# The last sum of a graph and expert layer: terms read in rows, the base kept in SBUF, the last two experts added by TensorE

## The reference

```python
xn = _layernorm(x)                                     # x: 625 rows of 512
x = x + gnn(xn, edges, ...) + mix(xn, ...)             # 10625 edges; linear attention, 8 heads
h = _layernorm(x)
x = x + ffn(h, ...)
# ffn: 64 experts, the 6 best of each row, and 2 shared experts
shared = sum over 2 of silu(h @ sWg) * (h @ sWu) @ sWd
top_w, top_i = top_k(softmax(h @ Wr), 6); top_w /= sum(top_w)
gate[n, top_i[n]] = top_w[n]
routed = sum over e < 64 of (silu(h @ Wg[e]) * (h @ Wu[e]) @ Wd[e]) * gate[:, e:e+1]
return shared + routed + h
```

## Time and profile before

| | us |
|---|---|
| time, median of 3 runs | 1015.66 |
| lowest and highest of them | 1013.46, 1018.88 |
| time of the profiled execution | 1019.58 |
| its span | 1017.5 |
| TensorE busy | 895.9 (88% of the span) |
| VectorE busy | 548.1 (54%) |
| ScalarE busy | 256.0 (25%) |
| GpSimd busy | 268.2 (26%) |

### The profile page before, as it was taken

How to read it: one execution, slowest core, us unless ns; L and a number is a source line. 1 busy time by engine, 2 the same in 40 slices (tenths; PEclk the granted TensorE clock), 3 DMA queues, 4 the chain that set the end, 5 groups by cost and what they waited for, 6 DMA issues and landing times. The chain is left out here.

```text
span 1017.5 us, 20833 instructions
## 1 busy us (share of the span) xinstructions
PE 895.9 (88%) x7497; PEld 589.3 (58%) x7497; DVE 548.1 (54%) x1623; ACT 256.0 (25%) x573; POOL 268.2 (26%) x265
## 2 busy tenths in 40 slices
PE   1599998897878298999999999999999989999991
PEld 1355555564544196676556566766676765656660
DVE  7997987978798986323324333334233332333216
ACT  2111101121130132333322322333233322322331
POOL 4543321334300102222222222222222322222211
PEclk9699999999989789999999999999999999999996
DMA  8856454565428951889979999999988999999976
GB/s 276 287 207 207 158 186 171 207 207 208 166 63 279 373 206 57 319 303 367 405 290 334 359 383 413 390 387 361 405 307 332 353 400 398 365 374 366 402 289 262
DMA packets 76929, 300.68 MB, mean 296 GB/s; under 512 B 13730, under 2 KB 14119, under 8 KB 58548
## 3 DMA queue, kind: packets, MB, share of 16 engines
q1 hardware_dynamic: 57256, 254.21, 65.9%
q0 software_dynamic: 17280, 38.48, 10.5%
q10 hardware_dynamic: 2252, 6.06, 1.7%
HBM read 290.26 MB, written 26.62 MB: 311 GB/s over the span
## 5 line engine op out<-in xcount | busy, mean ns | idle before, releaser
L1202 DVE TENSOR_TENSOR arena<-arena 128x288 f32 (+1 forms) x640 | 236.3, 449 | 37.8 <-remote 24.5
L1826 PE MATMUL bank<-arena,low 128*64 128x256 f32 x2048 | 241.6, 383 | 2.0 <-issue 2.0
L1667 PE MATMUL bank<-arena,multi 128*64 128x256 f32 x1296 | 162.0, 400 | 44.0 <-DVE arena L1202 32.6
L1826 PEld LDWEIGHTS bank<-arena,low 128*64 128x64 f32 x2048 | 141.0, 137 | 75.6 <-issue 12.4
L1851 PE MATMUL bank<-arena,low 128*64 128x256 f32 x1392 | 161.6, 379 | 1.1 <-ACT low L980 1.1
L1667 PEld LDWEIGHTS bank<-arena,multi 128*64 128x64 f32 x1296 | 99.5, 144 | 102.2 <-issue 44.2
L743 POOL DMA_INDIRECT low<-xr_d,idx x64 | 90.2, 1409 | 238.7 <-DVE place L1433 177.6
L747 POOL DMA_INDIRECT y_d<-low,place x64 | 68.5, 1070 | 262.3 <-ACT low L987 181.8
L1851 PEld LDWEIGHTS bank<-arena,low 128*64 128x64 f32 x1392 | 101.3, 137 | 50.3 <-ACT low L980 1.3
L987 ACT ACTIVATE low<-bank,gcol 64x256 f32<-64x256 f32 x174 | 82.1, 472 | 105.0 <-PE bank L1851 103.9
L687 POOL DMA_INDIRECT arena<-xn_d,ssel x79 | 90.3, 1143 | 38.2 <-issue 21.8
(11 more groups left out here) (214 smaller groups left out, 710.9 us busy)
## 6 DMA issues: line engine op xcount, KB each, us to landing
arena<-in_L_ffn_Wg_dram SPq DMA_DIRECT2D x64, 1024.0 KB
arena<-in_L_ffn_Wu_dram SPq DMA_DIRECT2D x64, 1024.0 KB
arena<-in_L_ffn_Wd_dram SPq DMA_DIRECT2D x64, 1024.0 KB
arena<-in_edge_attr_dram SPq DMA_DIRECT2D x88, 256.0 KB
arena<-y_d SPq DMA_DIRECT2D x5, 1250.0 KB, 6.8
sums_d<-arena ACTq DMA_DIRECT2D x18, 256.0 KB, 3.2
arena<-sums_d SPq DMA_DIRECT2D x4, 896.0 KB
arena<-in_L_mix_W_qkv_dram SPq DMA_DIRECT2D x2, 1024.0 KB, 18.1
```

What stands on the lines that cost most here:

```text
L1202: return dve.tensor_tensor(prod[:, buf, 0:n, EXT * p:EXT * p + EXT], x1[b][:, 0:n, bass.ds(i1, EXT)], x2[b][:, 0:n, bass.ds(i2, EXT)], ALU ...
L1667: ins = pe.matmul(bank[2 * b + c // 2][64 * h:64 * h + 64, 256 * (c % 2):256 * (c % 2) + 256], pair[:, pairs, i, :], prod[:, buf, i, 256 * ...
L1826: ins = pe.matmul(out_bank[64 * h:64 * h + 64, w * HF:(w + 1) * HF], xgT[:, b, k, 64 * o:64 * o + 64], gu[:, slot, w, k, h * HF:(h + 1) * HF],
```

## The change

- The base is neither stored nor loaded: `base_d` is gone. The first add reads `x_sb` and term 0 and writes `total`. Terms, total and output are handled by rows: 125 partitions x 5 tiles x 512 floats, in pieces of 2,048 bytes, each transfer in two DMAs (112 and 13 partitions).
- The scatters stop after expert 61 (`KEPT` = 2). The rows of experts 62 and 63 stay in `yy`. As they would have gone to terms 4 and 5, which then have rows that nothing writes, these two terms are set to zero in DRAM by SP in windows 6 and 7 of the first part.
- For each of the two experts VectorE makes a table `marks` of 128 x 625 ones and zeros (row `p` has a one where `idx[p]` is the token). At the end TensorE multiplies each table's five parts by `yy`, adding both experts in five banks; VectorE adds the banks to `total` before the last term.
- Term 4 now needs no scatter after that of expert 61. Term 5 goes to the buffer of term 0 and so waits for the first add. Buffers move accordingly.
- ScalarE clears rows 64 to 127 of both `yy` buffers ahead of the loop.
- The branch for overflow batches, not taken here, is adapted.

```diff
+TILE = TT * D
+KEPT = 2
-    m["terms"] = [arena[:, a:a + FLAT] for a in (4 * GU, 4 * GU + FLAT, 0, GU, 2 * GU, 3 * GU)]
+    m["terms"] = [arena[0:TR, a:a + TILE].rearrange("p (t d) -> p t d", t=TT)
+                  for a in (4 * GU, 4 * GU + TILE, 0, TILE, 2 * TILE, 4 * GU)]
+    m["zeros"] = low[:, 7728:7978]
+    m["marks"] = xT[:, 0:KEPT * N].rearrange("p (j n) -> p j n", j=KEPT)
+        FINAL_BANK = (7, 0, 1, 3, 2)
+        ENDS = ((0, 2), (2, 4), (4, TT))
...
+            def blank_term(i):
+                flat = y_d[i * N:(i + 1) * N, :].rearrange("n d -> (n d)").rearrange("(p j c) -> p j c", p=128, c=250)
+                sp.dma_start(flat, zeros[:, None, :].to_broadcast([128, 10, 250])).then_inc(s_blank, 16)
...
+                if w in (6, 7):
+                    blank_term(w - 2)
...
             def load_term(i):
-                rows = flat(y_d[i * N:(i + 1) * N, :])
-                if i < TOPK - 1:
-                    sp.dma_start(terms[i], rows).then_inc(s_term[max(i - 1, 0)], 16)
-                else:
-                    for j, (a, b) in enumerate(((0, HALF), (HALF, FLAT))):
-                        sp.dma_start(terms[i][:, a:b], rows[:, a:b]).then_inc(s_term[i - 1 + j], 16)
+                rows = y_d[i * N:(i + 1) * N, :].rearrange("(t p) d -> p t d", t=TT)
+                for a, b in PARTS:
+                    sp.dma_start(terms[i][a:b], rows[a:b]).then_inc(s_term[i], 16)
...
-                if e == FIRST_DONE - 1:
-                    store_base()
-                if e == FIRST_DONE + 1:
-                    sp.wait_ge(s_based, 32)
-                    sp.dma_start(total, flat(base_d)).then_inc(s_basef, 16)
...
-            for i in range(2, TOPK):
+            for i in (2, 3):
                 scattered(FIRST_DONE + i)
                 load_term(i)
+            load_term(TOPK - 2)
+            sp.wait_ge(s_added, 1)
+            load_term(TOPK - 1)
...
-            for i, (a, b) in enumerate(((0, HALF), (HALF, FLAT))):
-                sp.wait_ge(s_sum, i + 1)
-                sp.dma_start(flat(out)[:, a:b], total[:, a:b]).then_inc(s_out, 16)
+            for i, (lo, hi) in enumerate(ENDS):
+                sp.wait_ge(s_sum, TT + i + 1)
+                for a, b in PARTS:
+                    sp.dma_start(out_tiles[a:b, lo:hi], total[a:b, lo:hi]).then_inc(s_out, 16)
...
+            pool.memset(zeros, 0.0)
...
-            for e in range(NX + 1):
+            pool.wait_ge(s_blank, 32)
+            for e in range(NX + 1 - KEPT):
...
+            for b in range(2):
+                act.activation(yy[CAP:CAP2, b, :], iota[CAP:CAP2, 0:D], ACT.Copy, scale=0.0)
...
             def add_term(i, again):
...
-                dve.tensor_tensor(total, total, terms[i], ALU.add).then_inc(s_added, 1)
+                dve.tensor_tensor(total, x_sb[:, :, :] if i == 0 else total, terms[i], ALU.add).then_inc(s_added, 1)
+            def mark_rows(i):
+                at = idx_t[:, i % PLACES, 0:1]
+                then(dve, dve.tensor_copy(at, idx[:, i % PLACES:i % PLACES + 1]))
+                dve.tensor_scalar(marks[:, i % KEPT, :], iota[:, 0:N], at, None, ALU.is_equal).then_inc(s_marked, 1)
...
-            for j, (a, b) in enumerate(((0, HALF), (HALF, FLAT))):
-                dve.wait_ge(s_term[TOPK - 2 + j], 16)
-                dve.tensor_tensor(total[:, a:b], total[:, a:b], terms[TOPK - 1][:, a:b], ALU.add).then_inc(s_sum, 1)
+            for t in range(TT):
+                dve.wait_ge(s_final, t + 1)
+                dve.tensor_tensor(total[:, t, :], total[:, t, :], bank[FINAL_BANK[t]][0:TR, :], ALU.add).then_inc(s_sum, 1)
+            dve.wait_ge(s_sum, TT)
+            dve.wait_ge(s_term[TOPK - 1], 32)
+            for lo, hi in ENDS:
+                dve.tensor_tensor(total[:, lo:hi], total[:, lo:hi], terms[TOPK - 1][:, lo:hi], ALU.add).then_inc(s_sum, 1)
...
+            for j in range(KEPT):
+                pe.wait_ge(s_ys, NX - KEPT + 1 + j)
+                for t in range(TT):
+                    ins = pe.matmul(bank[FINAL_BANK[t]][0:TR, :], marks[:, j, t * TR:(t + 1) * TR], yy[:, (NX - KEPT + j) % 2, :],
+                                    start=(j == 0), stop=(j == KEPT - 1), skip_group_check=True)
+                    if j == KEPT - 1:
+                        ins.then_inc(s_final, 1)
```

More of the change, by code:

```diff
@@ L197, in gps_layer @@
         gu, dn, shgu, shdn, terms, total = m["gu"], m["dn"], m["shgu"], m["shdn"], m["terms"], m["total"]
+        zeros, marks = m["zeros"], m["marks"]
         iota = sb("iota", [128, 768])
@@ L581, in _ @@
                 load_up(e, wu[e])
-            base_tiles = base_d.rearrange("(t p) d -> p t d", t=TT)
-            def flat(rows):
-                return rows.rearrange("n d -> (n d)").rearrange("(p f) -> p f", p=128)
-            def store_base():
-                sp.wait_ge(s_shb, NS * TT)
-                for a, b in PARTS:
-                    sp.dma_start(base_tiles[a:b], x_sb[a:b]).then_inc(s_based, 16)
             def scattered(e):
@@ L642, in _ @@
                 sp.wait_ge(s_y, NX)
-                for i in (TOPK - 2, TOPK - 1):
-                    sp.wait_ge(s_term[i], 16)
+                for i in range(TOPK):
+                    sp.wait_ge(s_term[i], 32)
                 sp.wait_ge(c_tab, 1)
@@ L655, in _ @@
                 sp.wait_ge(s_routed, 1)
-                sp.dma_start(total, flat(base_d)).then_inc(s_basef, 16)
-                for i in range(TOPK):
+                for i in range(TOPK - 1):
                     load_term(i)
-            for i, (a, b) in enumerate(((0, HALF), (HALF, FLAT))):
-                sp.wait_ge(s_sum, i + 1)
-                sp.dma_start(flat(out)[:, a:b], total[:, a:b]).then_inc(s_out, 16)
-            sp.wait_ge(s_out, 32)
+                sp.wait_ge(s_added, TOPK)
+                load_term(TOPK - 1)
+            out_tiles = out.rearrange("(t p) d -> p t d", t=TT)
+            for i, (lo, hi) in enumerate(ENDS):
+                sp.wait_ge(s_sum, TT + i + 1)
+                for a, b in PARTS:
+                    sp.dma_start(out_tiles[a:b, lo:hi], total[a:b, lo:hi]).then_inc(s_out, 16)
+            sp.wait_ge(s_out, 32 * len(ENDS))
         @block.gpsimd
@@ L767, in _ @@
             with pool.If(0 < n_extra):
+                for i in range(TOPK):
+                    pool.wait_ge(s_term[i], 32)
+                for e in range(NX - KEPT, NX):
+                    pool.wait_ge(s_ys, e + 1)
+                    pool.wait_ge(s_place2, e + 1)
+                    scatter(e % PLACES, e % 2, s_scat[e % 2])
+                for b in range(2):
+                    pool.wait_ge(s_scat[b], 16 * (NX // 2))
                 pool.sem_inc(c_added, 1)
@@ L1484, in _ @@
                     index(i % PLACES).then_inc(s_place2, 1)
+                    if i >= NX - KEPT:
+                        mark_rows(i)
                     if i + 2 < NX:
@@ L1961, in _ @@
                         down(1, 0, bank[OV]).then_inc(c_y, 1)
-            pe.matmul(bank[0][0:1, 0:1], ident[:, 0:1], ident[:, 0:1], start=True, stop=True)
+                pe.wait_ge(s_marked, KEPT + 1)
+                pe.wait_ge(s_routed, 1)
+            pe.wait_ge(s_marked, KEPT)
+            pe.wait_ge(s_place2, NX)
+            pe.wait_ge(s_shb, NS * TT)
+            for j in range(KEPT):
[5 more added lines that the diff above has]
+                        ins.then_inc(s_final, 1)
 _INS = ['x', 'src', 'dst', 'edge_attr_512', 'L0_gnn_path_coeffs', 'L0_gnn_path_indices', 'L0_mix_W_qkv',
```

29 lines of the change are left out of this document (14 added, 15 removed).

## The result

The changed kernel takes 1028.67 us (median of 12 runs, 1024.81 to 1032.5), the kernel before 1016.73 us beside it (12 runs, 1013.46 to 1024.25). The ratio is 1.0109 with a 95% interval of 1.0091 to 1.0127: slower by 9 to 13 us, where 2.5 us more (1018.2) was forecast.

A forecast was written before the change was run, and what follows sets the result against it. TensorE bounds the expert loop, so only the tail behind it changes: its steps end at 1020.0 against 1017.5 us, and 1015.66 + 2.5 gives 1018.2 us. Range 1016.8 to 1019.2; 8 in 10, 1014.5 to 1021.3.

The forecast's parts named there:

- The loop's end: End of expert loop: VectorE's first large add starts right behind the loop's last product, at 993.24 us as before.
- When the terms are there: Tail, term loads: 3.4 us per term, term 4 landing near 1006.2 us, fifth large add ending at 1009.1.
- The adds from the banks and the last three: VectorE's tail: five bank adds of 0.69 us, 3.45 in all, then three adds for the last term, 3.15 us.
- The output: End of tail: six DMAs with data flowing in one row of 3.3 us, span ending at 1020.0 us.
- the 13 us of the old chain: Tail before: 7.89 us scatter of expert 63 plus 5.29 us last term's return; that chain alone suggested some 13 us gain.
- The zeros: SP's queue behind edge rows of windows 6 and 7: zeroing terms 4 and 5, cost 0, at most 4 us each.
- the base's traffic: Expert loop's full stretch: 2.56 MB of store and load removed, taken as 0 us, bounds 0 and -6.5.
- rival C: Expert loop: the base's traffic did hold it, up to 6.5 us earlier, 1011.7 us; chance 5%.
- D: Windows of the first part: zeros delay window gathers, up to 8 us, 1026 us at worst; chance 3%.
- Rival A: Tail: smaller pieces let the scatter of expert 61 through, no add waits, tail +0.9, 1016.6 us; chance 25%.
- Rival B: Ten table matmuls: TensorE's clock falls to 1.2 GHz, 1020.1 to 1021.6 us in the end; chance 12%.
- The slack of 2.7 us: Tail: TensorE's ten table matmuls end at 1007.4 us, 2.7 us before VectorE's first bank add at 1010.1.

The follow-up runs named there:

- e4: Changed kernel with terms 0 and 1 loaded behind the last down weights instead of ahead; 1032.73 us against 1015.05 for the kernel before, ratio 1.0185.
- e1: Changed kernel with each term loaded by one DMA of 128 partitions, same 2,048 B pieces; 1002.59 us against 999.15 for the kernel before, ratio 1.0039.
- e3: Changed kernel without the 13-partition DMA of each term load, so those rows lack their terms; 1004.54 us, ratio 1.0063 to the kernel before.
- e10: e9 with each term load as two DMAs of 64 partitions; 1015.72 us against 996.76 for the kernel before, ratio 1.0191.
- e6: e9 without VectorE's five adds from the banks, so rows of experts 62 and 63 are missing; 1017.25 us, ratio 1.0019 to the kernel before.
- e8: Kernel before the change, with its output stored from 112, 13 and 3 partitions; 1000.32 us, ratio 1.0016 to the kernel before.
- e9: e1 with term 2's load held back until the scatter of expert 61 has landed; 1023.73 us against 1015.05 for the kernel before, ratio 1.009.
- v3: e9 with the last term added by TensorE through an identity table, replacing VectorE's last three adds; 1022.8 us, ratio 1.0073 to the kernel before.
- v4: e9 with term 0 added inside the loop, count read earlier, bank adds between large adds, last term in two pieces; 1000.59 us against 997.01, ratio 1.0027.
- e2: Changed kernel with 10,240 B term pieces, still 112 and 13 partitions, terms added to wrong rows; 1008.94 us, ratio 1.0121 to the kernel before.
- e7: e1 with all 64 experts scattered, no tables, table matmuls or bank adds; 1001.98 us, ratio 1.0046 to the kernel before.

## Why the prediction was wrong

Its end of the span was 1020.0 us, the trace has 1027.9. The 7.9 us come from four places, in the order of the sum.

- **The loop's end** was taken as fixed. It is 0.46 us later, from slow terms ahead of weights in the queue (shown by e4 and by e1, whose products are back at 5.70 and 5.71 us).
- **When the terms are there: the step that failed.** The working said "a term now moves as pieces of 2,048 B ... so 1.28 MB takes 3.4 us and not 3.2". The term had the right place in the sum and the wrong size: 5.9 us. From the first large add to the memset the forecast has 16.9 us, the trace 23.2, so this stage costs 6.3 of the 7.9 us. Not all of it is the partitions: e1, with the forecast's 3.4 us a term, still takes 19.05 us for this stage. So 4.0 us of the 6.3 come from the slow packets. The other 2.2 lie in the working around them: the scatter took 7.95 us in e1 where I had 7.2, and from the issue of term 3 to the landing of term 4 it was 10.5 us (976.26 to 986.75) where I had allowed 9.1. Why the two terms need 1.4 us more than their data is open.

  For the 4.0 us the omission is plain. I looked at what the diff does to the pieces and not at what it does to the partitions, though `PARTS` stood in it, and took the price from edge rows, which go into 128 partitions. e1, e3 and e10 show it: same pieces, other partitions, 84, 120 to 141 and 147 ns. That the scatter of expert 61 landed after 5.1 us and not 7.2 in the changed kernel brought nothing, because the terms ahead filled the queue.
- **The adds from the banks and the last three** took 6.09 us from the memset on, 6.6 were forecast: 3.08 for 3.45, since five in a row come to 0.62 each where the single one took 0.69. The mechanism held, and e6 prices it at 3.0 us.
- **The output** took 4.89 us, 3.3 were forecast. e8 gives 1.5 us for splitting the stores, but by the later issue of the last DMA and not by a lower rate that one could see. The forecast let the data of six DMAs flow "in one row" from the first issue on and put nothing for issuing them; the last issue ends 2.3 us behind the last add.

What held: taking the last scatter and load out of the chain gained nothing, because VectorE was as late beside it; so the 13 us of the old chain were no gain. Full adds last 2.83 us for 2.82. The zeros, ScalarE's clears, the tables and the base's traffic are worth nothing that can be seen: the loop's rows stand where they stood, so rival C (a gain from the base) and D (late gathers) are both out. Rival A would have needed the quick scatter, which came only where no term was issued within a microsecond of it (2.6 to 3.4 us in e9, e6, v3, v4, e3 and e8). Rival B's clock did fall, to 0.66 in the mean of 1010 to 1015 us, after TensorE had stopped for 2.56 and 2.39 us; but the last bank add waited for the terms and not for TensorE, so it cost nothing. The slack of 2.7 us that I had counted there would not have covered the 13.1 us from 1001.93 to 1015.0, had the terms been on time.

The range's upper end, 1021.3, was too low because both bounds of a term came from transfers over 128 partitions. The trace of before does hold the new form: x is loaded in 112 and 13 partitions and 2,048 B pieces from 3.41 us on, 560 packets for the first part. SP's queue from 5 to 8 us:

```profile
q1 hardware_dynamic: 412, 0.84, 94.3%
```

That is 110 ns per packet, 40% above the price that I took, and what the changed kernel shows in its stretch from 994 to 998 us (111). It would have put a term at 3.4 x 110 / 78 = 4.8 us; two of them in a row are 2.8 us later, which is a forecast of 1021 and a range that reaches well beyond, still short of 142 ns but on the right side.

Two sums of the prediction are off by 0.1 us, which changes nothing: the output's row from 1015.6 to 1019.0 is 3.4 us and not 3.3, and rival B's three parts of 7.2 us lead from 1016.3 to 1023.5.

As to the change itself: even with its loads mended it gains nothing. It takes the last scatter and load out of a chain beside which VectorE was busy anyway, and puts 2.4 us onto VectorE and 1.5 onto the output. No complete version that was tried beats the kernel before; the nearest is v4 at 1.0027. A v4 whose output leaves from 128 partitions in two DMAs was not tried; by e8's 1.5 us its tail would be some 25.2 us (my estimate). That is 0.9 us above the 24.3 of the kernel before, less than the 1.0 us by which two profiles of that kernel's own instructions differ, so whether it would win or lose stays open.

## What to carry to other kernels

When a diff changes the shape of a transfer, compare the partitions before the bytes: price it from a row over the same partitions and from more than one stretch, and if none is in the trace, put double the price in the range. Count the DMAs behind the last result too, since each is issued after the one before. A tile of 125 rows is better padded to 128 in DRAM and loaded by one DMA than split into 112 and 13. And where two chains end together, taking work from one of them gains at most the difference between them; what is added to the other counts in full.

## What the runs showed of the hardware

- The same 2,048 B packet cost 84 ns over 128 partitions (e1), 120 to 141 over 112 (e3) and 147 over two halves of 64 (e10), with the DMA engines' share at or above 1.0 in all three. A full share says nothing of the rate: 399 GB/s in e1, 238 with the change, 224 in e10.
- Within one form the price rises as terms follow each other: 111 and then 148 ns with the change, 120 and then 141 in e3. Over 128 partitions it stays at 84 to 86 (e9).
- An output in five or six DMAs ended 4.9 to 5.0 us after the last add in e8, e1, e6, e7, e9 and v4, one in two DMAs 3.4; the last issue came 1.5 us later in e8.
- Packets of instructions took 0.9 to 1.1 us at the end of the kernel before and up to 1.7 with the change, but 1.8 also in e1, where the loads were quick and TensorE did not stop. TensorE stopped for up to 2.56 us with "issue" as the only reason given.
- The scatter of expert 61 landed 2.6 to 3.0 us after its issue with no term's load near it (e9, e6, v3, v4), and 3.0 to 3.4 with one issued over a microsecond behind it (e3, e8). With one issued within 0.7 us it took 6.0 to 8.0 (before, e1, e2, e7), and beside the slow split loads of the other runs 5.1 to 10.6.
- Five adds from banks in a row took 0.62 us each, a single one of the same form 0.69.
